# One attention stage in a new static order: maxima moved by DMA, short score tiles merged, one key transpose a group

## The chip, the cores and the metric

The kernel runs on one core of one Trainium2 chip. The metric is the time of one execution in microseconds, taken on the device; several executions are taken, and their median counts. The core has five engines with instruction streams of their own: TensorE (PE), VectorE (DVE), ScalarE (ACT), GpSimd (POOL) and SyncE (SP), which here only issues DMAs. They are ordered among each other by semaphores alone.

## The reference, cut to what matters

Two layers are computed over an input of 8 batches x 512 tokens x 128 features. The change is in the attention of the first:

```python
def _L0_attn_ref(x, Wk, Wq, Wv, Wo, bo, kln_w, kln_b, qln_w, qln_b):
    b, t, e = x.shape              # 8, 512, 128; x is layer-normed before
    h, s = 16, e // 16             # 16 heads of 8
    k = layernorm((x @ Wk).reshape(b, t, h, s), kln_w, kln_b)
    q = layernorm((x @ Wq).reshape(b, t, h, s), qln_w, qln_b)
    v = (x @ Wv).reshape(b, t, h, s)
    dot = einsum('bqhs,bkhs->bhqk', q, k) / sqrt(s)
    attn = softmax(where(causal, dot, -inf), axis=-1)
    return einsum('bhqk,bkhs->bqhs', attn, v).reshape(b, t, e) @ Wo + bo
```

Its result is added to `x` with that of a soft mixture of experts, whose last step (32 tiles of four matmuls, called "out" below) overlaps with the start of the attention. The second layer follows.

## The kernel before

Stage A projects queries, keys and values for all 32 token tiles of 128; stage C is the router and the experts; stage B is the attention. In B the 16 heads of a batch make four groups of four heads, so there are 32 groups in all, and a group has four query tiles and four key tiles of 128 tokens, in two pairs of heads each. For one group these items are done:

- `K`: SP turns the keys by DMA (`turn_keys`, line 656), four transposes of 128 x 256 bf16. The keys were split by POOL before (`nk`, seven steps a batch, lines 813 to 831; `nq` are the same for the queries, `nv` pads the values, `nb` adds the output bias).
- `Q`: PE turns the queries (eight transposes, line 2049), and ACT copies them to `qt1` (line 1652).
- `q` 0 to 7: scores with queries on the partitions, one unit for each query tile and pair of heads (lines 1993 and 1998, the second adds the causal mask); DVE takes each row's maximum from PSUM (`max_q`, line 1149).
- After `q` 7 DVE writes the negated maxima as two bf16 parts into two columns of each head in `qs` (`max_rows`, lines 1156 and 1157).
- `Z`: PE turns `qs` again, now with the maxima in it (line 2049), and ACT copies it to `qt2` (line 1652). The keys have ones in these two columns.
- `k` 0 to 7: scores the other way round, keys on the partitions (line 2009), which hold score minus maximum; ACT takes the exponential (line 1661).
- `m` 0 to 3: POOL zeroes what the causal mask excludes (line 794). `pv` 0 to 3: PE weighs the values (line 2023), ACT copies the sum (line 1667).
- `O`: PE turns the output (line 2062), DVE normalises it into `atok` (lines 1163 and 1168).

Once a batch `A` turns `atok` (line 2062, ACT copies it, line 1652) and `W` multiplies by `Wo` (line 2060); DVE adds the result to `x` and takes the statistics of the new rows (`residual`, lines 1177 to 1190).

PSUM has eight banks. The score units `q` and `k` go round three pairs of banks: PE may write a unit when the unit three places before has been read. `Q`, `Z`, `O`, `A` and `W` all go through bank 6, `pv` sums in bank 7.

The order is written out by hand. Each item has a time, in units of which a group has eight; the items sorted by time are the list, and every engine does its own items of it in that order and waits for each. The list covers two batches (eight groups) and is repeated as a round; items with a time under 16.5 belong to the round before. Before the attention's first round SP and the other engines bring the semaphores up to where a round before would have left them (`Skip`), and POOL's first normalisation waits for SP's.

## Time and profile before

| | us |
|---|---|
| median of 3 runs (lowest, highest) | 1042.38 (1042.19, 1045.29) |
| the profiled execution's own time | 1036.81 |
| span of its trace | 1035.1 |
| from the first to the last group's row maxima (line 1156) | 312.95 |
| mean granted TensorE clock | 0.949 |

The profile is one execution, with the start and length of every instruction on each engine and what released it after a wait. PE is matmuls, PEld the loading of their weights, and SPq the instructions in SP's queue. A busy share is an average over stages with different limits, and an engine's in-order stream means that one late item delays all behind it.

### The profile page before, as it was taken

The page shows a single profiled execution, that of the slowest core. Times are in us where ns is not written, and L with a number is a line of the kernel's source. Part 1 is how long each engine was busy: PE and PEld are TensorE (multiplying, and loading weights), DVE is VectorE, ACT ScalarE, POOL GpSimd, SP SyncE. Part 2 cuts the span into 40 slices and gives each one's busy share as a digit, 9 for nine tenths or more (in the row PEclk, how much of TensorE's full clock was granted, in tenths as well). Part 3 has the DMA queues.
Part 4 walks back from the last instruction along what each step waited for, and adds up shares of the span by engine and source line. Part 5 has one row for each costly group of instructions (what it writes and reads, how often), then busy time and mean ns, then how long its engine had stood idle before and what let it go on. Part 6 is the DMA issues. An engine that isn't in the chain of part 4 may idle for free.

```text
span 1035.1 us, 19063 instructions
## 1 busy us (share of the span) xinstructions
PE 857.0 (83%) x6870; PEld 557.6 (54%) x6870; DVE 708.6 (68%) x1512; ACT 583.8 (56%) x1091; POOL 563.6 (54%) x649
## 2 busy tenths in 40 slices
PE   7699979988899899899898587667888868999880
PEld 4366654467444444444444264345565547998870
DVE  6789963025778788787787459998767754465484
ACT  6566655410877788687787464344776652424220
POOL 2400007182586686686722149996127762888872
PEclk9999999999999999999999789988999998999995
DMA  5012212346111111111110199200101111232287
GB/s 151 1 77 86 83 82 60 95 142 189 23 30 28 24 30 29 24 33 24 28 29 7 50 165 288 61 1 1 41 14 54 43 44 64 87 103 76 75 235 205
DMA packets 111500, 74.59 MB, mean 72 GB/s; under 512 B 42626, under 2 KB 104524, under 8 KB 109360
## 3 DMA queue, kind: packets, MB, share of 16 engines
q1 hardware_dynamic: 101040, 64.05, 22.9%
q0 software_dynamic: 4608, 6.64, 1.9%
q10 hardware_dynamic: 5760, 2.70, 1.0%
q8 instruction: 55, 0.90, 0.4%
q14 instruction: 37, 0.30, 0.1%
HBM read 34.14 MB, written 33.70 MB: 66 GB/s over the span
## 4 chain that ended last, share of the span: by engine, by line
DVE 22%; PE 20%; POOL 14%; issue 11%; ACT 5%; DMA 2%; POOLq 0%; ACTq 0%; DVEq 0%
DVE B_mneg L1149 4%; PE banks L2023 4%; POOL y_dram L976 4%; ACT B_pt L1661 2%; PE banks L1993 2%; PE banks L2049 2%; PE banks L2009 2%; DVE D_dmx L1279 2%; PE banks L2158 2%; PE banks L2107 2%; DVE banks L1328 2%; POOL B_n L818 1%; DVE D_sc L1305 1%; PE banks L2062 1%; POOL x L952 1%
## 5 line engine op out<-in xcount | busy, mean ns | idle before, releaser
L1149 DVE TENSOR_REDUCE B_mneg<-banks 128x2 f32<-128x256 f32 (+3 forms) x256 | 205.4, 822 | 45.1 <-PE banks L1998 36.7
L1661 ACT ACTIVATE B_pt<-banks 128x1024 f32<-128x1024 f32 (+3 forms) x256 | 175.7, 709 | 65.8 <-PE banks L2009 63.6
L794 POOL TENSOR_SCALAR_AFFINE_SELECT B_pt<-B_pt 128x512 f32<-128x512 f32 x128 | 80.9, 634 | 131.3 <-ACT B_pt L1661 123.0
L2023 PE MATMUL banks<-B_pt,B_vp 128*32 128x512 f32 (+3 forms) x1024 | 96.3, 447 | 13.9 <-ACT B_ot L1667 6.9
L1811 ACT ACTIVATE F_gh<-banks 128x512 f32<-128x512 f32 (+1 forms) x96 | 49.4, 527 | 87.2 <-PE banks L2227 83.1
L931 POOL DMA_INDIRECT rows_dram<-F_xs,F_rowi x64 | 62.4, 976 | 59.4 <-issue 58.5
L1652 ACT COPY B_qt<-banks 128x1024 bf16<-128x1024 bf16 x64 | 64.7, 1011 | 40.9 <-PE banks L2049 39.7
L2158 PE MATMUL banks<-D_qk 128*128 128x512 f32 x128 | 74.3, 664 | 12.0 <-DVE D_pr L1290 12.0
L1993 PE MATMUL banks<-B_kt,B_qt 64*128 64x384 bf16 (+3 forms) x512 | 78.6, 304 | 5.1 <-DVE B_mneg L1149 2.5
L2009 PE MATMUL banks<-B_qt,B_kt 64*128 64x256 bf16 (+3 forms) x512 | 77.6, 304 | 4.7 <-ACT B_pt L1661 3.2
L976 POOL DMA_INDIRECT y_dram<-F_yo,F_ide x60 | 60.3, 1004 | 37.6 <-DVE F_yo L1507 17.4
L2235 PE MATMUL banks<-F_gw,F_gh 128*128 128x128 f32 x640 | 75.3, 275 | 0.2 <-DVE F_yo L1507 0.2
L2235 PEld LDWEIGHTS banks<-F_gw,F_gh 128*128 128x128 f32 x640 | 73.9, 192 | 1.1 <-DVE F_yo L1507 0.5
L917 POOL TENSOR_TENSOR D_prodv<-D_gex,D_q 128x64 f32<-128x64 f32 (+7 forms) x64 | 57.0, 933 | 13.2 <-ACT D_gex L1784 13.1
L1998 PE MATMUL banks<-B_mask_q,B_identb 64*128 64x128 bf16 (+1 forms) x512 | 63.6, 202 | 0.0
L1998 PE MATMUL banks<-B_mask_q,B_swapped 64*128 64x128 bf16 (+1 forms) x512 | 61.8, 202 | 0.0
L760 POOL CAST B_identb<-ident 128x128 bf16<-128x128 f32 x1 | 0.3, 290 | 110.3 <-ACT C_slotsT L1600 110.3
L1507 DVE TENSOR_TENSOR F_yo<-banks,F_she 128x512 f32<-128x512 f32 (+1 forms) x24 | 14.5, 602 | 61.9 <-POOL F_ide L961 44.1
L1279 DVE TENSOR_REDUCE D_dmx<-banks 128x1 f32<-128x512 f32 x64 | 43.7, 685 | 17.6 <-PE banks L2158 16.7
L1998 PEld LDWEIGHTS banks<-B_mask_q,B_swapped 64*128 64x128 bf16 x512 | 45.8, 95 | 12.4
L2009 PEld LDWEIGHTS banks<-B_qt,B_kt 64*128 64x128 bf16 x512 | 24.6, 93 | 50.1 <-issue 19.7
L897 POOL TENSOR_TENSOR D_prod<-D_q 128x128 f32<-128x128 f32 (+7 forms) x32 | 44.3, 1413 | 10.3 <-ACT D_q L1711 8.9
(295 smaller groups left out, 2173.7 us busy)
## 6 DMA issues: line engine op xcount, KB each, us to landing
comb_dram<-C_comb SPq DMA_DIRECT2D x8, 1024.0 KB, 3.8
C_cst<-comb_dram SPq DMA_DIRECT2D x8, 1024.0 KB, 5.0
rows_dram<-D_zeros SPq DMA_DIRECT2D x8, 650.0 KB, 15.7
F_xe<-rows_dram SPq DMA_DIRECT2D x8, 650.0 KB, 3.9
C_w<-w_in SPq DMA_DIRECT2D x16, 256.0 KB, 3.1
y_dram<-D_zeros SPq DMA_DIRECT2D x2, 2048.0 KB, 17.7
F_gw<-mw_in SPq DMA_DIRECT2D x16, 256.0 KB, 3.0
F_xs<-y_dram SPq DMA_DIRECT2D x16, 256.0 KB, 4.7
```

The lines of the kernel that those rows point to most:

```text
L794: g.affine_select(out=w, in_=w, compare_op=ALU.is_ge, fill=0.0, base=0, pattern=[[0, G], [1, P]], channel_multiplier=-1).then_inc(B_md, 1)
L976: pool.indirect_dma_start(out=(y_late[late] if late >= 0 else y_dram)[:, :], out_offset=bass.IndirectOffsetOnAxis(ap=ide[:, par, m:m + 1], ...
L1149: v.tensor_reduce(mneg[:, g % 2, qt, 2 * hp:2 * hp + 2], banks2[pair_of_banks(item)][:, :, 0:(qt + 1) * P], X, ALU.max, negate=True).then_ ...
L1279: v.tensor_reduce(dmx[:, u:u + 1], bank[2 + (n - 1) % 3][:], X, ALU.max, negate=True).then_inc(D_mx, 1)
L1652: a.copy(dst, bank[6][:] if kind == "A" else bank[6][:].bitcast(BF16)).then_inc(B_me, 1)
L1661: a.activation(pt[:, 2 * hp:2 * hp + 2, PT_AT[kt]:PT_AT[kt] + w], banks2[pair_of_banks(item)][:, :, 0:w], ACT.Exp).then_inc(B_ex, 1)
L1993: t_.matmul(banks2[ring][:, h, 0:(qt + 1) * P], qt1[HALF[h], g % 2, hp, qt * P:(qt + 1) * P], kt_[HALF[h], g % NG, 0:qt + 1, hp, :], start ...
L1998: ins = t_.matmul(banks2[ring][:, h, qt * P + half * QL:(qt + 1) * P], picks, mask_q[HALF[h], 0:P - half * QL], start=False, stop=(half == 1))
L2009: ins = t_.matmul(banks2[ring][:, h, 0:T - kt * P], kt_[HALF[h], g % NG, kt, hp, :], qt2[HALF[h], g % 2, hp, kt * P:T], start=True, stop=True)
L2023: ins = t_.matmul(bank[7][SL * r:SL * r + SL, kt * P:T], vp[:, g // NG, kt, SL * h:SL * h + SL], pt[:, r, PT_AT[kt]:PT_AT[kt] + T - kt * P ...
L2158: t_.matmul(bank[2 + (n - 1) % 3][:], qk[:, b % 2, h, t * P:(t + 1) * P], qk[:, b % 2, 2 + h, :], start=True, stop=True).then_inc(D_sf, 1)
L2235: ins = t_.matmul(bank[4 + alt][:, t * D:(t + 1) * D], gh[:, alt, m, t * P:(t + 1) * P], gw2[:, e, m, :], start=(m == 0), stop=(m == NJ - 1))
```

## The change

- The repeated round is dropped. One list (`B_PLAN`) holds the items of all 32 groups and the 32 "out" tiles, with new times. `Skip` and its semaphore counts go from this stage, and the key semaphores are waited for at 16 a group and not 64.
- `Z` goes. DVE writes the maxima of a group as 32 bf16 columns into a tile of their own (`mrow`); the new item `R` turns this tile (one transpose), ACT copies 32 partitions of 128 to `mrT`, and SP moves them by four DMAs into the rows of `qt` that stand for the maxima. The first `k` unit waits for these four. `qt` has a place for each of the four groups of a batch.
- The units of query tiles 0 and 1 hold both pairs of heads, and so do those of key tiles 2 and 3: six `q` and six `k` units a group where there were eight of each. The matmuls stay as they are, the maxima and exponentials of such a unit are one instruction.
- `K` is one DMA transpose of 128 x 1024. For this `qs`, `ks`, `vp`, `qkv` and `rst8` are laid out by group, and stage A writes them so.
- `nk` and `nq` have a normalising buffer each, their steps interleave, and the first two batches' steps don't wait for SP.
- In the new list `A` and `W` stand further behind `O`. `st` is written by the aggregation itself, without the copy of line 1190.

The order of PE in one group's period, by the new times: q5, pv0 (two groups back), q3, k5 (two back), k1 (one back), pv1, q2 (next group), k0, q4, R, pv2, k3, q0, pv3, O (three back), k2, q1, k4, Q (two ahead).

```diff
-OF_GROUP = {"q": (-0.6, 0.4, 2.0, 3.3, 3.7, 4.1, 5.1, 7.0), "k": (11.4, 12.4, 14.3, 15.3, 16.3, 17.6, 18.6, 19.0),
-            "m": (14.8, 17.1, 18.4, 20.4), "pv": (15.8, 18.7, 21.9, 22.3), "K": (-8.7,), "Q": (-4.0,), "Z": (9.9,), "O": (24.1,)}
-OF_BATCH = {"nk": (-34.0, -33.6, -32.8, -31.3, -26.6, -26.3, -23.3), "nq": (-23.1, -20.0, -19.0, -17.6, -16.5, -15.4, -13.6),
-            "nv": (-8.1,), "nb": (-13.5,)}
-OF_LAST_GROUP = {"A": 27.2, "W": 29.7}
+GROUPS = B * NG
+QUNITS = ((0, (0, 1)), (1, (0, 1)), (2, (0,)), (2, (1,)), (3, (0,)), (3, (1,)))
+KUNITS = ((0, (0,)), (0, (1,)), (1, (0,)), (1, (1,)), (2, (0, 1)), (3, (0, 1)))
+UNITS_OF = ((0, 1), (2, 3), (4,), (5,))
+
+OF_GROUP = {"K": (-17.95,), "Q": (-8.22,), "q": (-2.64, -1.48, -3.99, 1.48, -3.76, 0.3), "R": (4.89,),
+            "k": (12.09, 10.22, 14.41, 13.26, 14.95, 17.71), "m": (22.44, 25.29, 27.45, 28.1),
+            "pv": (17.26, 19.83, 21.02, 21.43), "O": (30.16,)}
+OF_BATCH = {"nk": (-29.73, -21.65, -19.43, -16.07, -11.11, -9.19, -8.75),
+            "nq": (-34.65, -34.63, -31.38, -23.28, -21.64, -16.54, -14.54), "nv": (20.36,), "nb": (-0.71,)}
+OF_LAST_GROUP = {"A": 34.63, "W": 41.99}
+OUT_FROM, OUT_STEP = -24.24, 1.115
...
-                    for t in range(NT):
-                        c0 = (g % NG) * 2 * P
-                        sp.dma_start_transpose(kt_[:, g % NG, t], ks[:, g // NG, t, c0:c0 + 2 * P]).then_inc(B_kt[g % NG], 16)
+            def turn_keys(g):
+                b = g // NG
+                if g % NG == 0:
+                    sp.wait_ge(B_ks, b + 1)
+                if g >= NG:
+                    sp.wait_ge(B_s2, B_PLAN.nth("k", *LAST_K[g - NG]))
+                sp.dma_start_transpose(kt_[:, g % NG].rearrange("p t a k -> p (t a) k"),
+                                       ks[:, b % 2, g % NG].rearrange("p t c -> p (t c)")).then_inc(B_kt[g % NG], 16)
+
+            def place_max_rows(g):
+                sp.wait_ge(B_me, B_PLAN.nth("misc", "R", g, 0))
+                for h in range(2):
+                    for part in range(2):
+                        r0, to = (2 * h + part) * 2 * NT, h * QL + MAX_AT + part
+                        sp.dma_start(qt[to:to + 1, g % NG].rearrange("p a t k -> p (a t) k"),
+                                     mrT[r0:r0 + 2 * NT, g % 2, :]).then_inc(B_rw[g % 2], 16)
...
+                if len(pairs) == 2:
+                    v.tensor_reduce(mneg[:, g % 2, :, :, qt_], scores[:, :, 0:2 * w].rearrange("p h (a k) -> p h a k", a=2),
                                     X, ALU.max, negate=True).then_inc(B_mx, 1)
...
-                    rows = qs[:, g // NG, :, :].rearrange("p t (h s) -> p t h s", s=QL)[:, :, G * (g % NG):G * (g % NG) + G, :]
-                    own.link(v.tensor_copy(rows[:, :, :, MAX_AT], mneg[:, g % 2, :, :]))
-                    v.tensor_tensor(rows[:, :, :, MAX_AT + 1], mneg[:, g % 2, :, :], rows[:, :, :, MAX_AT],
-                                    ALU.subtract).then_inc(B_m, 1)
+                low = mneg[:, g % 2].rearrange("p h a t -> p h (a t)")
+                own.link(v.tensor_copy(mrow[:, g % 2, :, 0, :], low))
+                v.tensor_tensor(mrow[:, g % 2, :, 1, :], low, mrow[:, g % 2, :, 0, :], ALU.subtract).then_inc(B_m, 1)
...
-                    own.link(v.tensor_copy(st[:, bass.ds(i0, NT), :], mv[:]))
...
+                elif kind == "R":
+                    if g >= 2:
+                        act.wait_ge(B_rw[g % 2], 64 * (g // 2))
+                    ins = a.copy(mrT[0:8 * NT, g % 2, :], bank[6][:].bitcast(BF16)[0:8 * NT, 0:P])
...
+                if len(pairs) == 2:
+                    a.activation(pt[:, :, PT_AT[kt]:PT_AT[kt] + w].rearrange("p (a h) q -> p h a q", a=2),
+                                 scores[:, :, 0:2 * w].rearrange("p h (a q) -> p h a q", a=2), ACT.Exp).then_inc(B_ex, 1)
...
+                if item == FIRST_K[g]:
+                    pe.wait_ge(B_rw[g % 2], 64 * (g // 2 + 1))
...
+                elif kind == "R":
+                    pe.wait_ge(B_m, g + 1)
+                    ins = t_.transpose(halves[0:8 * NT, 0:P], mrow[:, g % 2].rearrange("p h s r -> p (h s r)"), identb[:])
```

## Rows read from the trace of the kernel before

**Rows 1.** The page, part 1: busy us, share of the span, instructions.

```profile
PE 857.0 (83%) x6870; PEld 557.6 (54%) x6870; DVE 708.6 (68%) x1512; ACT 583.8 (56%) x1091; POOL 563.6 (54%) x649
```

**Rows 2.** Windows: stretch, length, busy of PE, PEld, DVE, ACT, POOL, PEclk, DMA, GB/s.

```profile
396.50:477.20 80.70, 72.34 (x953) 36.35 (x952) 65.36 (x117) 62.01 (x90) 58.09 (x72) 1.00 0.14 28
```

**Rows 3.** Timeline of DVE, line 1156 alone: start us, us.

```profile
252.76 0.21 DVE L1156 CAST B_qs<-B_mneg 128x16 bf16<-128x16 f32 x1
...
396.48 0.21 DVE L1156 CAST B_qs<-B_mneg 128x16 bf16<-128x16 f32 x1
...
405.11 0.52 DVE L1156 CAST B_qs<-B_mneg 128x16 bf16<-128x16 f32 x1
...
423.50 1.10 DVE L1156 CAST B_qs<-B_mneg 128x16 bf16<-128x16 f32 x1
...
437.34 0.20 DVE L1156 CAST B_qs<-B_mneg 128x16 bf16<-128x16 f32 x1
...
565.71 0.20 DVE L1156 CAST B_qs<-B_mneg 128x16 bf16<-128x16 f32 x1
```

**Rows 4.** Timeline of all engines at the end of a batch.

```profile
425.86 0.65 PE L2062 MATMUL banks<-ident,B_atok 128*128 128x128 f32 x4 [0.38 <-DVEq L1171]
...
427.19 1.16 PE L2060 MATMUL banks<-wo,B_aT 128*128 128x128 f32 x8 [0.68 <-ACT B_aT L1652]
...
428.38 0.69 DVE L1177 TENSOR_TENSOR x<-banks,x 128x512 f32<-128x512 f32 x1 [2.07 <-PE banks L2060]
...
429.19 0.62 PE L2049 MATMUL banks<-B_identb,B_qs 128*128 128x128 bf16 x8 [0.63 <-DVEq L1178]
...
431.19 0.69 DVE L1149 TENSOR_REDUCE B_mneg<-banks 128x2 f32<-128x512 f32 x1
```

**Rows 5.** Lines, forms apart, 396.5 to 477.2: busy us, mean ns | idle before.

```profile
L1149 DVE TENSOR_REDUCE B_mneg<-banks 128x2 f32<-128x1024 f32 x16 | 19.5, 1220 | 1.0 <-PE banks L1998 0.2
L1661 ACT ACTIVATE B_pt<-banks 128x1024 f32<-128x1024 f32 x16 | 16.5, 1028 | 1.5 <-PE banks L2009 1.0
L1652 ACT COPY B_qt<-banks 128x1024 bf16<-128x1024 bf16 x16 | 16.2, 1011 | 1.3 <-PE banks L2049 0.9
...
L1149 DVE TENSOR_REDUCE B_mneg<-banks 128x2 f32<-128x512 f32 x16 | 11.1, 692 | 8.4 <-PE banks L1998 8.4
...
L1661 ACT ACTIVATE B_pt<-banks 128x512 f32<-128x512 f32 x16 | 8.9, 595 | 13.4 <-PE banks L2009 13.4
...
L1149 DVE TENSOR_REDUCE B_mneg<-banks 128x2 f32<-128x256 f32 x16 | 6.7, 422 | 1.5 <-DVE B_atok L1168 0.5
...
L1661 ACT ACTIVATE B_pt<-banks 128x256 f32<-128x256 f32 x16 | 6.2, 386 | 0.6 <-PE banks L2009 0.5
...
L1156 DVE CAST B_qs<-B_mneg 128x16 bf16<-128x16 f32 x9 | 4.3, 480 | 0.3
```

**Rows 6.** Timeline of PE: the eight transposes and what follows, and one pv.

```profile
400.60 0.62 PE L2049 MATMUL banks<-B_identb,B_qs 128*128 128x128 bf16 x8
...
401.16 0.34 PE L1993 MATMUL banks<-B_kt,B_qt 64*128 64x384 bf16 x2
...
408.08 0.85 PE L2023 MATMUL banks<-B_pt,B_vp 128*32 128x384 f32 x8
```

**Rows 7.** DMA issues: count, KB each, median us from issue to landing.

```profile
B_kt<-B_ks SPq DMA_TRANSPOSE x128, 2.4
...
D_lam<-lams_in SPq DMA_DIRECT2D x4, 64.0 KB, 2.7
```

**Rows 8.** Tile B_kt: ns min/median/max of one issue in SP's queue.

```profile
L656 SPq DMA_TRANSPOSE B_kt<-B_ks x128: 1167/1246/2573, 212.9 to 543.7; - x128
```

**Rows 9.** Timeline of SP behind the attention.

```profile
589.26 1.85 SPq L672 DMA_DIRECT2D D_lam<-lams_in  x4
```

**Rows 10.** Timelines of POOL and PE before the attention.

```profile
203.38 1.07 POOL L813 TENSOR_TENSOR B_n<-qkv,rst 128x512 f32<-128x512 f32 x1 [26.92 <-SPq L135]
...
219.53 7.38 PE L1965 MATMUL banks<-C_eo,C_cst 128*128 128x128 f32 x64 [0.97 <-ACT C_eo L1639]
```

More of the change, by code:

```diff
@@ L209 @@
 OUT_FIRST = sum(bank_ < 4 for bank_ in OUT_BANK)
-def b_items(first, last):
-    if first:
-        return FIRST_ROUND
-    return [item for item in B_ROUNDS.order if not (last and item in EARLY)]
 def pair_of_banks(unit):
-    return B_ROUNDS.streams["unit"].index(unit) % 3
+    return B_PLAN.streams["unit"].index(unit) % 3
 OF_ROUTER = {"g": (-5.3,), "x": (-3.6,), "l": (-0.6, -0.3, 0.5, 0.6), "u": (1.2, 4.2, 3.0, 8.1),
@@ L381, in build @@
         eps, root = sb("eps", [P, 1]), sb("root", [P, 1])
-        turns = sem("turns")
         s_x = [sem(f"x_in{c}") for c in range(4)]
@@ new lines, in residual @@
+            def residual(b, stats=True):
+                dve.wait_ge(B_mf, B_PLAN.nth("misc", "W", b, 0))
+                dve.wait_ge(B_bo, b + 1)
+                i0 = b * NT
+                xb = x[:, i0:i0 + NT, :].rearrange("p t d -> p (t d)")
+                own.link(v.tensor_tensor(xb, bank[6][:], xb, ALU.add))
+                dve.sem_inc(B_me, 1)
+                if not stats:
+                    return
+                for t in range(NT):
+                    ins = v.bn_stats(bn6[:, t, :], x[:, i0 + t, :])
+                own.link(ins)
+                for t in range(NT):
+                    ins = v.bn_aggr(st[:, i0 + t, :], bn6[:, t, :])
+                own.link(ins)
@@ L1228, in second_deviations_of @@
                 own.link(v.reciprocal(rst2[:, tiles], var2[:, tiles]))
-            dve_round(-1, True)
-            for it in range(B // 2 - 1):
-                dve_round(it, False)
-            dve_round(B // 2 - 1, False, True)
+            for item in B_PLAN.order:
+                kind, g, i = item
+                if kind == "out":
+                    add_experts(g, i)
+                elif kind == "q":
+                    max_q(g, i)
+                    if item == LAST_Q[g]:
+                        max_rows(g)
+                elif kind == "O":
+                    normalise(g)
+                elif kind == "W" and g == B - 1:
+                    deviations_of(FIRST_BATCHES, 1)
+                    residual(g, stats=False)
+                elif kind == "W":
+                    residual(g)
             dve.sem_inc(B_end, 1)
@@ new lines, in weigh_values @@
+            def weigh_values(item):
+                _, g, kt = item
+                pe.wait_ge(B_md, B_PLAN.nth("m", "m", g, kt))
+                if kt == 0:
+                    if g % NG == 0:
+                        pe.wait_ge(B_v, g // NG + 1)
+                    if g:
+                        pe.wait_ge(B_ot, g)
+                for r in range(G):
+                    ins = t_.matmul(bank[7][SL * r:SL * r + SL, kt * P:T],
+                                    vp[:, g // NG % 2, g % NG, kt, SL * r:SL * r + SL],
+                                    pt[:, r, PT_AT[kt]:PT_AT[kt] + T - kt * P], start=(kt == 0), stop=(kt == NT - 1))
+                ins.then_inc(B_pv, 1)
@@ new lines, in _ @@
+            pe.wait_ge(B_const, 1)
+            for item in B_PLAN.order:
+                kind, g, i = item
+                if kind == "out":
+                    sum_experts(g, i)
+                elif kind == "q":
+                    scores_q(item)
+                elif kind == "k":
+                    scores_k(item)
+                elif kind == "pv":
+                    weigh_values(item)
+                elif kind in ("Q", "R", "O", "A", "W"):
+                    through_bank_6(item)
```

549 lines of the change are left out of this document (212 added, 337 removed).

## Prediction

> **What bounds the kernel now.** The page came first [rows 1]: PE is busy for 83% of the span, DVE for 68%, and no other engine leads, so the split by stage decides. The windows over the attention of stage 1 show it as periodic: a stretch of 80.70 us, eight groups, has PE busy for 72.3, DVE for 65.4, ACT for 62.0 and POOL for 58.1, at a granted clock of 1.00, and the stretch before it is the same to 0.2 us [rows 2]. PE is idle for 8.4 us of the 80.7, and no engine is full. So it is a schedule in which four engines between 72% and 90% wait for each other in turn, and what the change is worth is read from its rhythm, not from one engine's load.
>
> The rhythm is in the timeline of DVE: line 1156 runs once a group, when the row maxima of the group are complete [rows 3]. The first is at 252.76 and the last at 565.71 us, 31 intervals in 312.95 us, 10.10 us a group. The two intervals from 405.11 to 423.50 take 18.39, 9.2 each; those in which a batch is finished take longer: 423.50 to 437.34 is 13.84. The one of the batch before ends at 396.48; as the round is 80.70 and its other six intervals are 8.6 to 9.3 (the two shown, and the one of 8.63 from 396.48 to 405.11), it takes about 12.4. Batch ends thus cost about 3.3 and 4.8 us over an ordinary interval of 9.07, 8.1 us a round.
>
> The timeline of the 13.84 us interval says why [rows 4]: A (atok turned, line 2062) starts at 425.86, W (the projection, line 2060) at 427.19 after a wait of 0.68 for the copy of A's result, the residual on DVE at 428.38 after DVE has sat idle for 2.07, and the next Q (line 2049) at 429.19 after another 0.63. O, A, W and the residual stand next to each other in the order of PE and share bank 6, so all queued behind them waits: scores, then maxima, then exponentials.
>
> **The change, part by part.**
>
> *The end of a batch.* In the new list O stands at 30.2, A at 34.6 and W at 42.0, where it was 24.1, 27.2 and 29.7 (a group is 8 of these units). Other units of work now lie between each, so the waits of [rows 4] go, and the work itself stays. On PE that is A (0.65) and W (1.1 to 1.2), on DVE 2.8 us from the residual at 428.38 to the next maximum at 431.19 [rows 4]. The copy of line 1190 and its gap go from that. I leave 2.2 us for each batch end, DVE's part, since DVE and PE are both near the path. So 8.1 us a round becomes 4.4: 1.85 us for each of the 7 batch ends inside the stretch, 13.0 us. Bounds: nothing, if the new order makes another wait, and 4.05 x 7 = 28 us, if this work hides as well.
>
> *Z goes, R comes.* Z turned the queries a second time, with the maxima in them. Eight transposes take PE from 400.60 to the next matmul at 401.16, 0.56 us [rows 6], and ACT copies 1,024 columns in 1.01 us [rows 5]. R is one transpose (0.07, an eighth) and a copy of 128 columns on 32 partitions: between nothing and the 0.39 of the shortest exponential (256 columns); I take 0.3. PE gains 0.49 us a group, ACT 0.7.
>
> *Merged units.* Of the sixteen units of a group four go. DVE: 2 x 0.422 becomes 0.692, 2 x 0.692 becomes 1.220, 0.32 us less. ACT: 2 x 0.595 becomes 1.028, 2 x 0.386 becomes 0.595, 0.34 us less [rows 5]. The matmuls are as many as before. With a ring of three bank pairs PE hands over twelve times and not sixteen. The CAST of line 1156 means 0.48 and once took 1.10 [rows 3, 5], against 0.21 at its shortest; I give it no gain, with at most 0.27 us a group as its other bound.
>
> What a group gains in time: no single engine is the path, so the least relief of the three bounds what is sure (DVE 0.32) and the relief of PE (0.49) is the rate at which it can go on when fed. The fewer hand-overs add something that no row prices. I take 0.5 us a group, 31 x 0.5 = 15.5 us. Bounds: 0, if the waits keep their pattern; and, if PE never idles, a round of 72.2 - 8 x 0.49 = 68.3 us, that is 12.4 less than 80.70 for both parts together, 48 us over 31 groups.
>
> *The maxima by DMA.* Behind R and its copy SP issues four DMAs of 2 KB, and the first k of the group waits for all. Four issues in a row on SP took 1.85 us [rows 9]. Their landing isn't in the trace in this form; the nearest rows are 2.4 us (the key transposes, also from SBUF to SBUF) and 2.7 (64 KB from HBM) [rows 7]. Chain: transpose 0.2, on ACT up to 1.0 behind an exponential, copy 0.3, three issues 1.4, landing 2.4 from the start of the fourth issue: 5.3 us. In the new order thirteen of a group's eighteen pieces of PE work lie between R and that k. Outside it are only k, pv 1, q, k, q: one pv of 0.85 [rows 6] and four units of about 0.3 (the two matmuls of one took 0.34 in the row of 384 columns), 2.0 us. At 8.6 us a group (9.07 less 0.5) that leaves 6.6 us. 5.3 is hidden, with 1.3 us to spare, so I cost it at nothing. Uncovered it costs PE its lateness in every group. The Trainium skill, DMA: Bandwidth & Descriptors, section Anatomy of one DMA, puts the fixed part of a DMA at about 2.0 us (its fit is of DMAs issued by GpSimd); by it the chain would be an estimated 4.9 us, and the room 1.7.
>
> *One key transpose for four.* An issue occupies SP for 1.246 us in the median, four for 5.0 [rows 8]. One of four times the size takes between 1.25 and 5.0 us. Nothing waits for it soon: it is issued when the fourth group back has finished its k units (unit 17.7 - 32 = -14.3), and the first q is at -4.0, ten units or some 11 us later. But it stands on SP ahead of the next R. That R's copy is ready some 3.5 us after the k unit that releases the transpose, so with 5 us of issue R is 1.5 us late, with 1.25 not at all. I take nothing; at 5 us the 1.3 us to spare just about goes.
>
> *Head and tail.* POOL starts the first normalisation at 203.38 after 26.92 us in wait for SP; the new order drops that wait, but PE begins the 32 expert tiles only at 219.53 [rows 10] and they run as many as before, so this is worth 0. In the order both have about the same number of units ahead of the first k; I take 0 there, plus or minus 3. At the end no q is left to hide the last R: its chain is 5.3 us where Z's was 0.62 and 1.01 [rows 5, 6], 3.7 more, part of it under what is left of group 30. I add 2.0. Stage A writes the same elements in another layout, 0.
>
> *POOL* keeps its work, 58.1 us of a round of 73 [rows 2]. It would be the next bound after PE.
>
> Sum: -13.0 - 15.5 + 2.0 = -26.5 us. The profiled execution took 1036.81 us (span 1035.1), so 1010.3; it lay 5.6 under the median of 1042.38, and against the median this is **1016 us**. The round should be 80.7 - 3.7 - 4.0 = 73.0 us.
>
> **The rivals.**
>
> *The full gain.* PE waits hardly at all, rounds near 70 us. For: the waits of [rows 4] are most of its idle time. Against: DVE and POOL are then near 90% of the round. Some 10.7 x 31 / 8 = 41 less, with the tail 39: 1003 us, down to 994.
>
> *Only the batch ends.* The order has its waits elsewhere, ordinary intervals stay at 9.07. For: ring and in-order waits, not load, set them. -13.0 + 2.0: 1031 us.
>
> *No net change*, POOL's masks come late behind the normalising steps, which the new list puts two at a time between them. For: POOL's busy share rises from 72% to 80%. Against: in the new order pv 0 stands five units behind the k units that its mask needs. 1042 us.
>
> *The maxima are late (slower).* Place: the first k of each group, waiting for the four DMAs. It decides when the chain is over 6.6 us by more than 0.9: the other gains are then used up, 26.5 / 31. So at a chain of 7.5 us, 2.2 more than my sum: landings of 4.6 us, or 3 us behind the transpose and 1.5 us of slower issue together. At 8.3 us it is 1.7 x 31 = 53 less 26.5, 1068 us. Against: no landing of a small transfer in the trace is over 2.7 [rows 7]. For: nothing like a write of eight rows into one partition is in it. The Trainium skill, DMA: Bandwidth & Descriptors, section Queues, rings and completion order, says that descriptors of one ring are consumed in order: the rows' would then stand behind the keys' of the same queue. No run here shows that.
>
> **How the numbers follow.** Forecast 0.40 (1007 to 1024), full gain 0.20, batch ends only 0.20, no change 0.07, late maxima 0.13. The range, 994 to 1041, takes in the first three and leaves out 0.20. Within 0.3%, 3.1 us, is about what a measurement of this kernel can't tell from no change. Faster 0.80, same 0.07, slower 0.13.
>
> **What the profile after would show.** The intervals between row maxima: 8.6 ordinary, about 10.8 at a batch end. A round at PE 68, DVE 61 to 63, ACT 54, POOL 57 busy. No wait of PE for the rows' DMAs but in the last group, and PE not waiting between A and W. DMA rows: issue to landing near 2.4 for the maxima; one transpose on SP of 1.25 to 5 us. Wrong would be: PE waiting for a DMA at the k line in each group, or ordinary intervals of 9 us with the masks as releaser.

## The result, and the profile after

The changed kernel takes 981.91 us in the median of 4 runs (978.41 to 987.38), the kernel before 1042.29 in the runs beside it (4, 1039.33 to 1045.29): ratio 0.9425, interval 0.9368 to 0.9483, 60 us less. The forecast was 1016 and its range began at 994, so the sign was right and the size was not: the sum had 26.5 us and the range at most 48. Each trace is of one execution, and the one to be read with care is that of e5_merge_old_order below, a slow execution of 1117.36 us where its fast ones take 1091 to 1098, but at a granted clock of 1.00 in the stage and with its excess behind the last mark, where it has 532 us and the other experiments 509 to 519.

The spans of the two profiled executions, 1035.1 and 976.7, differ by 58.4. The row maxima, the mark of [rows 3], say where that lies (timeline of DVE of the changed kernel, line 1119 alone: start, duration):

```profile
250.89 0.17 DVE L1119 CAST B_mrow<-B_mneg 128x16 bf16<-128x16 f32 x1
...
350.72 0.18 DVE L1119 CAST B_mrow<-B_mneg 128x16 bf16<-128x16 f32 x1
...
359.98 0.45 DVE L1119 CAST B_mrow<-B_mneg 128x16 bf16<-128x16 f32 x1
...
367.69 0.45 DVE L1119 CAST B_mrow<-B_mneg 128x16 bf16<-128x16 f32 x1
...
375.90 0.28 DVE L1119 CAST B_mrow<-B_mneg 128x16 bf16<-128x16 f32 x1
...
383.92 0.18 DVE L1119 CAST B_mrow<-B_mneg 128x16 bf16<-128x16 f32 x1
...
507.75 0.45 DVE L1119 CAST B_mrow<-B_mneg 128x16 bf16<-128x16 f32 x1
```

31 intervals in 256.86 us, 8.29 us a group, where there were 312.95 and 10.10: 56.1 of the 58.4 us are inside the stage. The first mark is 1.9 us earlier, and from the last mark to the end of the span it is 469.0 us where it was 469.4. The repeating batch is 9.26, 7.71, 8.21 and 8.02: an ordinary group takes 7.98, and a batch end costs 1.28 over that. In before these were 9.07 and 4.05. In the terms of the forecast's sum: ordinary groups 34 us (forecast 15.5), batch ends 19.4 (13.0), and the rest, 5 us, at and beyond the two ends of the stage.

The windows over eight groups, to be set beside [rows 2] (length, then busy of PE, PEld, DVE, ACT, POOL, the granted clock, DMA share, GB/s):

```profile
334.50:400.90 66.40, 63.26 (x900) 31.81 (x896) 62.57 (x99) 54.28 (x75) 56.76 (x65) 1.00 0.21 35
```

The round was to be 73.0 us and is 66.4. It is even below the 68.3 that I gave as the round in which PE never idles, and PE still idles 3.1 of it. PE and DVE are now busy for 95% and 94%. On the page of the whole span PE went down by 37 us from [rows 1]:

```profile
PE 820.4 (84%) x6646; PEld 538.7 (55%) x6646; DVE 694.8 (71%) x1441; ACT 551.9 (57%) x1027; POOL 558.3 (57%) x617
```

The lines of this stretch with forms apart (busy us, mean ns, idle just before them), beside [rows 5]:

```profile
L1112 DVE TENSOR_REDUCE B_mneg<-banks 128x2 f32<-128x1024 f32 x16 | 19.4, 1214 | 0.0
...
L1109 DVE TENSOR_REDUCE B_mneg<-banks 128x4 f32<-128x1024 f32 x8 | 9.8, 1226 | 1.2
...
L1623 ACT ACTIVATE B_pt<-banks 128x1024 f32<-128x1024 f32 x8 | 8.1, 1018 | 0.0
L1603 ACT COPY B_qt<-banks 128x1024 bf16<-128x1024 bf16 x8 | 8.1, 1018 | 0.0
...
L1109 DVE TENSOR_REDUCE B_mneg<-banks 128x4 f32<-128x512 f32 x8 | 5.4, 678 | 0.0
...
L1623 ACT ACTIVATE B_pt<-banks 128x512 f32<-128x512 f32 x8 | 4.8, 597 | 3.2 <-PE banks L1952 3.2
```

The joined tiles last as long as the sum said: 1,226 and 678 ns for the two joined maxima, 1,018 and 597 for the two joined exponentials. The idle time before the 512-column forms, 8.4 us on DVE and 13.4 on ACT in [rows 5], is 0.0 and 3.2.

The end of a batch, beside [rows 4] (timeline of all engines):

```profile
341.97 0.66 PE L1996 MATMUL banks<-ident,B_atok 128*128 128x128 f32 x4
...
349.73 1.16 PE L1999 MATMUL banks<-wo,B_aT 128*128 128x128 f32 x8
...
351.03 0.68 DVE L1140 TENSOR_TENSOR x<-banks,x 128x512 f32<-128x512 f32 x1
```

No row has a wait: the 0.68 before W and the 2.07 before the residual are gone. And the maxima on their way (timeline of PE, ACT and SP of one group):

```profile
344.21 0.23 PE L1989 MATMUL banks<-B_identb,B_mrow 128*32 128x128 bf16 x1
...
344.94 0.24 ACT L1607 COPY B_mrT<-banks 32x128 bf16<-32x128 bf16 x1
...
345.20 2.67 SPq L642 DMA_DIRECT2D B_qt<-B_mrT  x4
...
350.82 0.39 PE L1952 MATMUL banks<-B_qt,B_kt 64*128 64x512 bf16 x2
```

R stands at 344.21, the issue of the fourth DMA begins at about 347.2, and the first k, at 350.82, waits for nothing. The view of line 642 and the tile view of the keys (ns min/median/max of one issue; then who waited, us and times):

```profile
L642 SPq DMA_DIRECT2D B_qt<-B_mrT x128: 634/635/1272, 254.1 to 512.6; - x128
...
  PE banks L1952: 1.4, 3
```

```profile
L634 SPq DMA_TRANSPOSE B_kt<-B_ks x32: 1232/1232/2190, 223.2 to 491.9; - x32
```

PE waits for the maxima's DMAs three times in 32 groups, 1.4 us in all.

### The profile page after: what moved, and what is told of

Its sections match the earlier page's. It is cut to its first block, busy times and chain, and to the rows that moved or that the text cites. A ratio compares the mean times of both kernels' runs of the same rounds, so it can differ in the third digit from the quotient of the medians.

```text
span 976.7 us, 18288 instructions
## 1 busy us (share of the span) xinstructions
PE 820.4 (84%) x6646; PEld 538.7 (55%) x6646; DVE 694.8 (71%) x1441; ACT 551.9 (57%) x1027; POOL 558.3 (57%) x617
## 4 chain that ended last, share of the span: by engine, by line
PE 37%; DVE 25%; POOL 13%; issue 10%; DMA 3%; ACT 3%; SPq 1%; ACTq 0%; POOLq 0%; DVEq 0%
PE banks L1965 5%; POOL y_dram L937 4%; PE banks L1934 3%; DVE B_mneg L1112 3%; PE banks L1952 3%; PE banks L1884 3%; PE banks L1878 2%; PE banks L1911 2%; DVE D_dmx L1228 2%; DVE C_nmax L1050 2%; PE banks L1856 2%; PE banks L1939 2%; PE banks L2086 2%; DVE banks L1277 2%; PE banks L2035 2%
## 5 line engine op out<-in xcount | busy, mean ns | idle before, releaser
L1112 DVE TENSOR_REDUCE B_mneg<-banks 128x2 f32<-128x768 f32 (+1 forms) x128 | 136.3, 1086 | 7.8 <-PE banks L1939 4.2
L1627 ACT ACTIVATE B_pt<-banks 128x768 f32<-128x768 f32 (+1 forms) x128 | 117.1, 917 | 31.8 <-PE banks L1952 30.0
L1934 PE MATMUL banks<-B_kt,B_qt 64*128 64x256 bf16 (+3 forms) x512 | 72.7, 301 | 1.7 <-ACT B_pt L1627 1.2
L1952 PE MATMUL banks<-B_qt,B_kt 64*128 64x256 bf16 (+3 forms) x512 | 64.7, 300 | 8.5 <-DVE B_mneg L1112 5.3
L1109 DVE TENSOR_REDUCE B_mneg<-banks 128x4 f32<-128x512 f32 x64 | 61.0, 953 | 4.8 <-PE banks L1939 0.5
L1623 ACT ACTIVATE B_pt<-banks 128x1024 f32<-128x1024 f32 x64 | 51.5, 809 | 12.7 <-PE banks L1952 12.7
L1939 PE MATMUL banks<-B_mask_q,B_identb 64*128 64x128 bf16 (+1 forms) x512 | 58.4, 202 | 0.0
L1939 PE MATMUL banks<-B_mask_q,B_swapped 64*128 64x128 bf16 (+1 forms) x512 | 57.1, 202 | 0.0
L1934 PEld LDWEIGHTS banks<-B_kt,B_qt 64*128 64x128 bf16 x512 | 24.8, 94 | 56.3 <-DVE B_mneg L1109 25.2
```

The source lines that it names most:

```text
L1112: v.tensor_reduce(mneg[:, g % 2, :, pairs[0], qt_], scores[:, :, 0:w], X, ALU.max, negate=True).then_inc(B_mx, 1)
L1627: a.activation(pt[:, 2 * hp:2 * hp + 2, PT_AT[kt]:PT_AT[kt] + w], scores[:, :, 0:w], ACT.Exp).then_inc(B_ex, 1)
L1934: t_.matmul(scores[:, h, n * w:(n + 1) * w], qt[HALF[h], g % NG, hp, qt_, :], kt_[HALF[h], g % NG, 0:qt_ + 1, hp, :], start=True, stop=False)
L1939: ins = t_.matmul(scores[:, h, n * w + qt_ * P + half * QL:(n + 1) * w], picks, mask_q[HALF[h], 0:P - half * QL], start=False, stop=(half ...
L1952: ins = t_.matmul(scores[:, h, n * w:(n + 1) * w], kt_[HALF[h], g % NG, kt, hp, :], qt[HALF[h], g % NG, hp, kt:NT, :], start=True, stop=True)
```

## The experiments

Fifteen kernels. Where they ran, the kernel before takes 1091 to 1096 us and not 1042, and the changed kernel 1022 (e8) and not 982. The extra time is not in the attention stage: there the changed kernel keeps its rhythm (8.28 and 8.29 us a group), and behind the last mark e8 has 517 us at a granted clock of 0.86, where the first trace had 469 at 0.90. So each ratio is against before on the same chip, and what tells the kernels apart best is the mean interval between row maxima, in us a group. A difference in it, times 31, is what it makes inside the stage.

Three cautions. Before was not traced there, so its 10.10 is that of the first trace; the ratios lie 0 to 1.6% below what the intervals give (e1, with 10.08 us a group, has 0.988), and what before loses there isn't explained. The experiments are best compared with each other. The granted clock of the stage is 1.00 in most of these kernels, but 0.98 in e13, 0.97 in e4, 0.96 in e2, 0.95 in e14 and 0.86 in e15, so a part of what these lose can be the clock. And all fifteen keep the changed kernel's layout by group and its normalising buffers; "old" is the order and the work alone.

| kernel | order | units a group | us a group | ratio (interval) |
|---|---|---|---|---|
| before | old, by rounds | 16 | 10.10 | 1 |
| e1_one_list_old | old, one list | 16 | 10.08 | 0.988 (0.982 to 0.994) |
| e5_merge_old_order | old, one list | 12 | 10.51 | 1.006 (1.001 to 1.011) |
| e14_split_later | old, later half moved | 16 | 13.22 | 1.089 (1.081 to 1.096) |
| e13_joined_later | old, later half moved | 12 | 11.47 | 1.029 (1.020 to 1.037) |
| e15_new_work_old_times | old, new work | 12 | 13.76 | 1.100 (1.091 to 1.109) |
| e2_old_work_new_order | new | 16 | 10.91 | 1.016 (1.010 to 1.023) |
| e4_split_new | new | 16 | 10.82 | 1.010 (1.005 to 1.015) |
| e11_join_q_only | new | 14 | 9.57 | 0.983 (0.972 to 0.995) |
| e9_split_spread | new, halves apart | 16 | 9.48 | 0.982 (0.971 to 0.993) |
| e10_five_spare | new | 12 | 8.93 | 0.967 (0.954 to 0.980) |
| e3_z_added | new | 12 | 8.64 | 0.952 (0.945 to 0.959) |
| e12_aw_tight | new, A and W close | 12 | 8.47 | 0.952 (0.941 to 0.963) |
| e6_two_drains | new | 12, drained in two | 8.35 | 0.935 (0.923 to 0.947) |
| e7_two_spare | new | 12 | 8.33 | 0.941 (0.929 to 0.952) |
| e8_changed_again | new | 12 | 8.28 | 0.932 (0.921 to 0.944) |

**The list, and the order.** The first four kernels undo parts of the change. e1 is the old work at the old times, sorted into one list without rounds:

```
-B_ROUNDS = Rounds(item_times(), AHEAD, PG, 8 * PG, {
+B_PLAN = Plan(b_item_times(), {"unit": "qk", "q": "q", "k": "k", "m": "m", "pv": ("pv",), "misc": "QROAW"})
```

> The old work (second turn Z, sixteen units a group, four key transposes) and the old times, but in one list for all 32 groups. Theory A, that the edge of the repeated round is what sets A and W of every second batch side by side at the end of the list: the intervals of 13.8 us become 12.4, four of them, about 1036 us, ordinary intervals stay at 9.1. Theory B, that the edge costs nothing: 1042 us and the same intervals as before.

10.08 us a group: nothing inside the stage. The batch end, by turns 13.84 and about 12.4 us before, is 12.25 in the repeating batch, and the other groups take 8.62, 9.89 and 9.53, where they had 9.07 on average: what the edge gives comes back as longer groups. e2 puts the old amount of work into the new order:

```
-QUNITS = ((0, (0, 1)), (1, (0, 1)), (2, (0,)), (2, (1,)), (3, (0,)), (3, (1,)))
+QUNITS = KUNITS = tuple((t, (hp,)) for t in range(4) for hp in range(2))
+                    for k in range(1, 2 * NT):
+                        t_.transpose(halves[:, k * P:(k + 1) * P], swapped[:], identb[:])
+                    ins = a.copy(unused[:, P:], bank[6][:].bitcast(BF16)[:, P:])
+                for t in range(NT):
+                    sp.dma_start_transpose(kt_[:, g % NG, t], ks[:, b % 2, g % NG, t, :]).then_inc(B_kt[g % NG], 16)
```

> The changed kernel with the old work put back: sixteen units a group (the halves of a merged unit next to each other), four key transposes, and seven more transposes and a copy of 896 columns at R, of a constant, in place of what Z did; the maxima still go by DMA. If the order makes most of the gain (theory order): 8.9 to 9.3 us a group with batch ends in it, 1005 to 1020 us. If the work taken out makes most of it (theory work): 9.8 a group, 1030 to 1035.

10.91 us a group, slower than before. It falls outside both theories (8.9 to 9.3, and 9.8). The new order without the new work is worth less than nothing when the halves of a short tile stand side by side; e9 below moves them apart.

**The work of Z.** e3 keeps the changed kernel and adds what Z had over R: seven more transposes (of a constant) and a copy of 896 columns.

> The changed kernel with seven more transposes on PE (of a constant) and a copy of 896 columns on ACT at R, the work of the second turn Z. If PE is the path: 0.48 us a group and more, 997 to 1000 us. If DVE is: at most 0.2 a group, 982 to 988.

8.64 against 8.28: 0.36 us a group, 11 us, between the two theories. In the sum it was a part of the 0.5 that I took for a group, with 0.49 of relief on PE. This price holds in the changed kernel only: e2 has this work and the four key transposes over e4 (next), and takes 0.1 us a group more.

**The joined tiles.** e4 is the changed kernel with sixteen units, both halves of a short tile side by side, and all else as changed.

> The changed kernel with sixteen units a group, the halves of each merged unit next to each other in the list. By my prediction's sum (DVE 0.32, ACT 0.34, PE nothing): about 10 us more, 992. If merging also relieves PE, as the fall of its busy time by 1.1 us a group says: 16 to 25 us more, 998 to 1007.

10.82 us, where the two theories expected 10 and 16 to 25 us: against its own split the joining is worth 2.53 us a group, 78 us, more than the whole change. e4's windows (as above), its chain of units (timeline of all engines) and its waits of PE (waited for: us, times, longest):

```profile
300.00:400.00 100.00, 79.58 (x1017) 38.69 (x1015) 77.25 (x128) 65.08 (x103) 63.23 (x73) 0.97 0.15 26
```

```profile
343.38 0.61 PE L1933 MATMUL banks<-B_kt,B_qt 64*128 64x512 bf16 x2
...
344.19 1.23 DVE L1111 TENSOR_REDUCE B_mneg<-banks 128x2 f32<-128x1024 f32 x1 [1.56 <-PE banks L1938]
...
345.64 0.96 DVE L1111 TENSOR_REDUCE B_mneg<-banks 128x2 f32<-128x768 f32 x1 [0.23 <-PE banks L1938]
...
346.66 0.39 PE L1951 MATMUL banks<-B_qt,B_kt 64*128 64x512 bf16 x2 [0.95 <-DVE B_mneg L1111]
...
350.38 0.23 PE L1933 MATMUL banks<-B_kt,B_qt 64*128 64x128 bf16 x2 [0.54 <-DVE B_mneg L1111]
```

```profile
PE banks L1951 <- DVE B_mneg L1111: 9.5, 9, 1.7
PE banks L1933 <- DVE B_mneg L1111: 5.0, 9, 0.7
PE banks L1951 <- ACT B_pt L1626: 4.3, 9, 0.5
```

Over the whole stage the 2.53 us are 1.73 of more idle time on PE and 0.80 of more busy time (its granted clock means 0.97). No engine is full, and PE stands for 18.8 us of 100 until DVE or ACT has drained a pair of banks. At 346.66 the wait ends 0.06 us after the maximum at 345.64 does. The same gaps return in each group. (The Trainium skill, Perfetto Trace Analysis, section Optimization Strategy, says of such a gap that it "can mean there isn't enough SBUF/PSUM for the next tile to be allocated (buffer count, tile sizes)"; here the trace agrees, with the releasers above.)

Is it the places in the ring or the instructions? e6 leaves the joined tiles in one pair of banks but drains them by two instructions, as before:

```
-                    v.tensor_reduce(mneg[:, g % 2, :, :, qt_], scores[:, :, 0:2 * w].rearrange(...), X, ALU.max, negate=True)
+                    for hp in range(2):
+                        ins = v.tensor_reduce(mneg[:, g % 2, :, hp, qt_], scores[:, :, hp * w:(hp + 1) * w], X, ALU.max, negate=True)
```

(and likewise for the exponential).

> The changed kernel, its short tiles still joined in one bank pair, but the joined unit read by two maxima on VectorE and two exponentials on ScalarE, one for each head pair, as before had them. So the instructions of the kernel before are back on both engines (four more a group) and the places in the ring are as in the changed kernel. Theory A, that instructions are what the joining saves: as slow as the split kernel, some 10.8 us a group, 1.01 of before. Theory B, that places and hand-overs are what it saves: the four instructions cost at most what they are, 0.3 us a group, so 8.3 to 8.7 us a group and 0.94 to 0.955 of before.

8.35 us, 0.07 over the changed kernel, or 2 us of 1,000. Its window is that of the changed kernel, PE 95% busy:

```profile
300.00:400.00 100.00, 95.12 (x1337) 47.05 (x1334) 94.75 (x171) 82.33 (x135) 85.48 (x98) 1.00 0.20 35
```

So the instructions, the one thing that I had priced, are worth 0.07 us a group here, and what is left of the 2.53 goes with the unit's place in the ring. Two things come with that place and aren't told apart here: its hand-over (e6 still signals once a unit), and that PE writes four matmuls in a row, which takes it less busy time (see the floor below). Two more kernels share this out. e9 has sixteen units again, with the second halves moved away from the first:

```
-            "q": (-2.64, -2.64, -1.48, -1.48, -3.99, 1.48, -3.76, 0.3)
-            "k": (12.09, 10.22, 14.41, 13.26, 14.95, 14.95, 17.71, 17.71)
+            "q": (-2.64, -0.6, -1.48, -0.2, -3.99, 1.48, -3.76, 0.3)
+            "k": (12.09, 10.22, 14.41, 13.26, 14.95, 18.9, 17.71, 19.3)
```

> The changed kernel with sixteen units a group as in e4_split_new (1.010 of before, 10.82 us a group), but the second halves of the four formerly joined short tiles are moved away from the first, into the stretches of the order that hold few units (query tiles 0 and 1: 2.0 and 1.3 us behind their first halves, mirror tiles 2 and 3: 4.0 and 1.6 us behind). Theory A, four more places taken in a ring of three cost their hand-overs wherever they stand: 10.3 us a group or more, 0.99 or more. Theory B, only the two short halves side by side stall it, since they give TensorE nothing to do while VectorE and ScalarE drain: 8.3 to 9.3 us a group, 0.935 to 0.965. Half way, 9.3 to 10.3, would leave both a part.

> The changed kernel with query tiles 0 and 1 joined as it has them and mirror tiles 2 and 3 in two units each, side by side: fourteen units a group. Splitting both cost 2.5 us a group (e4_split_new). Theory A, each place of the ring costs the same: +1.25 us a group, 9.5 us, 0.97 to 0.98 of before. Theory B, the long chain of the mirror tiles (ScalarE drains them at 0.7 to 1.2 us, and waits for the maxima) is what the split hits: +2 us or more, 10.3 us, 0.99 or more. Theory C, the query side: +0.5 us at most.

e9 takes 9.48 us: half of the cost goes when the halves stand apart, half stays (0.78 of idle time on PE and 0.42 of busy time). Sixteen units in this order are thus 0.6 us a group faster than before. e11, with two of the four joins undone, takes 9.57, half of e4's loss: what its first theory said, the same price a place (0.96 idle, 0.32 busy). The waits of PE in e9 and e11, in 100 us each:

```profile
PE banks L1933 <- ACT B_pt L1626: 7.0, 13, 0.6
PE banks L1951 <- DVE B_mneg L1111: 3.9, 12, 0.5
```

```profile
PE banks L1952 <- DVE B_mneg L1112: 9.7, 11, 1.0
PE banks L1952 <- ACT B_pt L1627: 4.1, 10, 0.4
```

**Joined tiles in the old order.** e5 is e1 with twelve units:

```
-            "q": (-0.6, 0.4, 2.0, 3.3, 3.7, 4.1, 5.1, 7.0), "k": (11.4, 12.4, 14.3, 15.3, 16.3, 17.6, 18.6, 19.0)
+            "q": (-0.1, 2.6, 3.7, 4.1, 5.1, 7.0), "k": (11.4, 12.4, 14.3, 15.3, 16.9, 18.8)
```

> The work of the kernel before (whole query tiles turned behind the maxima, four key transposes a group), its order times, one list for all groups, and short tiles 2 and 3 of the first matrix and short tiles 0 and 1 ... of the mirror image joined: six units and six units where before had eight and eight. To be set beside e1_one_list_old, which differs from it only in the joining (0.988 of the kernel before, 10.08 us a group). Theory A, the joining is worth its instructions only (some 0.34 us of ScalarE and 0.32 of VectorE a group, under 0.4 us a group): 0.975 to 0.99 of before, 9.6 to 10.1 us a group. Theory B, the joining frees places in the ring of three bank pairs that the score tiles pass through, and these hand-overs set the pace in any order: 8.7 to 9.3 us a group, 0.93 to 0.95 of before. Theory C, it frees them but only the new order can use it: 9.4 to 10.0 us a group here.

10.51 us, slower than e1 and outside all three theories; the whole times agree in direction, 1093 us against 1086. PE's waits in 100 us:

```profile
PE banks L1979 <- DVEq L1122: 8.1, 10, 1.4
PE banks L1952 <- ACT B_ot L1622: 3.8, 7, 0.5
```

It doesn't wait for the ring, but for the row maxima at Z (line 1979). I took the chain behind the last query tile for the cause, and gave it more room in e13 and e14: Z later by 0.7, mirror tiles and all that follows by 1.2.

> e5_merge_old_order (old work and old order times, short tiles joined, 10.51 us a group) with everything behind the maxima later in the order: R by 0.7 of the eight units of a group, mirror tiles, their products with V, the output transposes and what follows by 1.2. In e5 TensorE waited at R for the maxima of the last query tile, 8.1 us in 100, and hardly for the ring. Theory A, the old order cannot use joined tiles because this chain ends last in it: with more room for it 9.2 to 10.0 us a group. Theory B, the joined units are bad in the old order by where they stand in it: 10.3 us or more.

> The same shift for the kernel with sixteen units (e1_one_list_old, 10.08 us a group), in which TensorE waited at R for only 2.6 us in 100 and for the ring for 3.9. Theory A, here the ring is the edge and the chain is not: 9.9 to 10.1 us, no gain. If it falls as much as e13, the room behind R was worth the time in either case, and joining is not what makes use of it.

The theory behind the two fell. The shift costs 1.0 us a group with joined tiles (11.47) and 3.1 without (13.22, where 9.9 to 10.1 was expected): with split tiles PE now waits for pairs of banks for 24.6 us in 100, with joined ones for 8.3. In e13 the wait at Z is down to 3.5 us in 100, and another has come first, that of the products with V for the masks:

```profile
PE banks L1951 <- POOL B_pt L767: 5.5, 4, 1.9
...
PE banks L1978 <- DVEq L1121: 3.5, 9, 0.4
```

So the chain was not what to relieve. e13's 11.47 lies where the second theory had it, but not for its reason: the joined units are not what is bad in that order, since between e14 and e13, otherwise the same, joining is worth 1.75 us a group.

**The way of the maxima.** e7 and e10 put two and five spare DMAs of 2 KB, to DRAM, ahead of the four on SP, so that these are issued 1.3 and 3.2 us later.

```
+                for i in range(2):
+                    sp.dma_start(spare[2 * g + i], mrT[0:2 * NT, g % 2, :]).then_inc(B_sp[g % 2], 16)
```

> The changed kernel with two spare DMAs of 2 KB on SyncE's queue, in each group, ahead of the four that move the maxima: at 0.635 us an issue they land 1.3 us later. Theory A, the chain of the maxima has some 3 us left before the first mirror tile: nothing (0.94 to 0.95, 8.3 us a group). Theory B, the chain is the edge already in each group: +1.3 us a group on 31 groups, some +40 us, 0.98.

> The changed kernel itself once more, so that the others of this call have it on their chip: 0.937 to 0.948 of before, 8.29 us a group, by every theory.

> As e7_two_spare (which took 8.33 us a group against 8.28 without them) with five spare DMAs ahead of the four that move the maxima: these land 3.2 us later. Theory A, the chain of the maxima has some 3 us left: 0 to +0.7 us a group, so under +20 us. Theory B, the slack is about 1.3 us, and everything beyond it goes into each group: +1.9 us a group, +60 us, 0.99 of before.

8.33 and 8.93 us: 1.3 us of lateness cost 0.05 us a group, 3.2 us cost 0.65. The waits of PE in e10, in 100 us, show the edge reached in five of some eleven groups:

```profile
PE banks L1959 <- DVE B_mneg L1118: 5.7, 6, 1.0
PE banks L1959 <- DMA B_qt<-B_mrT: 4.9, 5, 1.4
```

e15 has the new work at the old times, with the first k only 1.5 behind R.

> The work of the changed kernel whole (joined tiles, one key transpose, the maxima alone turned and moved by DMA) in the order times of before, in which the first mirror tile stands 1.5 behind R in place of 5.3. The four DMAs with their copy take some 3.9 us to the landing. Theory A, a late landing goes into each group almost whole, as my slower rival had it: 11 to 12 us a group, 1.01 to 1.06 of before. Theory B, TensorE finds other work and half of it is hidden: 10 to 11 us.

13.76 us a group, 3.7 more than before, beyond what either theory allowed. The chain in the open (timelines of PE and SP, then PE's waits in 100 us):

```profile
339.34 0.23 PE L1988 MATMUL banks<-B_identb,B_mrow 128*32 128x128 bf16 x1 [0.42 <-DVEq L1132]
...
340.14 3.09 SPq L641 DMA_DIRECT2D B_qt<-B_mrT  x4
...
344.44 0.47 PE L1951 MATMUL banks<-B_qt,B_kt 64*128 64x512 bf16 x2 [3.38 <-DMA B_qt<-B_mrT]
```

```profile
PE banks L1951 <- DMA B_qt<-B_mrT: 23.1, 8, 3.4
```

From R to k it takes 5.10 us. Over the whole stage this wait comes 32 times and takes 90.8 us, 2.8 us a group. In this kernel the granted clock also means 0.86 over the stage, so the 3.7 us are not all the wait itself.

**A and W.** e12 moves both close behind the last O again, as they were.

```
-OF_LAST_GROUP = {"A": 34.63, "W": 41.99}
+OF_LAST_GROUP = {"A": 33.26, "W": 35.76}
```

> The changed kernel, with the transposes of the attention result and the product with the output weights put back close behind the transposes of the last group (1.4 and 2.5 us between the three instead of 4.5 and 7.4), as before had them at the end of a batch. My prediction held that this row of turns through one bank costs 3.6 us of a batch end, 13 us with the round's edge for all of them. Theory A, it does: +2 to +3.5 us a batch, +15 to +28 us. Theory B, with one list other work lies between them in any case: under +1 us a batch, within 0.7% of the changed kernel.

8.47 us, 0.19 us a group or 6 us for all batch ends, 0.8 a batch: its second theory. But its four intervals are 7.47, 7.46, 9.55 and 9.52, so its batch ends cost 4.1 us over an ordinary group, as in before, and its ordinary groups are half a microsecond shorter than the changed kernel's. Read so, moving A and W apart mostly spreads the same delay over the batch. The waits come back (timeline of PE), but they are small:

```profile
344.48 0.66 PE L1996 MATMUL banks<-ident,B_atok 128*128 128x128 f32 x4 [1.16 <-ACT B_qt L1603]
```

## Why the prediction was wrong, step by step

**The step that failed** is the price of the merged units: "The fewer hand-overs add something that no row prices. I take 0.5 us a group." I priced the joining by its instructions and took the hand-overs for a small addition. It is the other way round. e6 puts the instructions at 0.07 us a group; e4, e9 and e11 put the four places of the ring at 2.5 us with the halves side by side, 1.2 with them apart. That alone is 37 to 78 us, where the sum had 15.5 for everything a group gains, and where ordinary groups did gain 1.09 us each, 34 us. The instructions were oversized as well: I took 0.32 us a group on DVE and 0.34 on ACT from the rows, and e6 has 0.13 and 0.12 more of them (busy time by form, whole stage).

Why a place is dear can be seen in e4, though only as an estimate. A large query tile is filled from 343.38 and drained at 345.42 (344.19 and 1.23): it holds its pair for 2.04 us. The ring has three pairs, so the fourth unit finds a free pair without waiting only if three units take at least that long to pass. By an estimate from the measured rhythm, three of twelve units pass in 3/12 x 8.29 = 2.07 us, three of sixteen would pass in 3/16 x 8.29 = 1.55. So twelve units just fit at the changed kernel's pace, and for sixteen three places last 2.0 us at 3/16 x 10.8, the pace of e4. This is no limit that was measured: 2.04 us is one large unit and not the mean, and e9 runs sixteen units at 9.48 us, 1.78 for three of them. It says that the ring is tight, not where it ends, and that where short and long units stand matters as much. What shows the ring at work is PE's waits, 18.8 us of 100 in e4 and 10.9 in e9. In before they are small, so there the ring is not what sets the pace (waits of PE, 300 to 400 us):

```profile
PE banks L2023 <- POOL B_pt L794: 2.8, 5, 0.8
PE banks L2049 <- DVEq L1171: 2.4, 9, 0.3
...
PE banks L1993 <- DVE B_mneg L1149: 0.8, 1, 0.8
...
PE banks L2009 <- DVE B_mneg L1149: 0.7, 2, 0.3
```

It comes up when the order is made denser. The eight banks leave no room for a fourth pair, so a longer ring, the direct test, was not run.

**The order and the joining don't add up.** The old order with joined tiles is 10.51 (as I placed them), the new order with split ones 10.82 or, with the halves apart, 9.48, both together 8.29, neither 10.08. A sum of parts, each priced in the kernel before, can't find 56 us of which one part has nothing alone and the other 19 at best (e9, with Z's work already gone). Here the parts were costed as independent, and that is the error behind the number. Shown is that the 8.29 needs both; the twelve-unit versions of the old order that I tried (e5, e13) had their waits at the row maxima and at the masks, and that no good order with the old spacing of maxima and mirror tiles exists isn't shown.

**The floor** was wrong as well: "if PE never idles, a round of 72.2 - 8 x 0.49 = 68.3" (with the 72.34 of [rows 2] it is 68.4). PE's busy time fell by 9.1 us a round, 1.13 a group, not 0.49. "The matmuls are as many as before" was true and didn't mean that their busy time is. The lines of PE over 300 to 400 us, first before, then after:

```profile
L2009 PE MATMUL banks<-B_qt,B_kt 64*128 64x512 bf16 (+3 forms) x160 | 24.3, 303 | 0.7 <-DVE B_mneg L1149 0.7
L1993 PE MATMUL banks<-B_kt,B_qt 64*128 64x512 bf16 (+3 forms) x156 | 23.9, 303 | 1.0 <-DVE B_mneg L1149 0.8
```

```profile
L1934 PE MATMUL banks<-B_kt,B_qt 64*128 64x384 bf16 (+3 forms) x194 | 27.6, 301 | 0.0
...
L1952 PE MATMUL banks<-B_qt,B_kt 64*128 64x128 bf16 (+3 forms) x196 | 24.7, 298 | 3.5 <-DVE B_mneg L1112 2.2 <-DMA B_qt<-B_mrT 0.5
```

A group has sixteen of each. One matmul lasts the same, 0.30 us, but they overlap: the sixteen of the mirror image occupied 24.3 / 160 x 16 = 2.43 us and now 24.7 / 196 x 16 = 2.02, those of the queries 2.45 and now 2.28. With some of them four in a row into one pair, they overlap more than two and two; e4, split again in the new order, is back at 21.9 / 148 x 16 = 2.37 for those of the mirror image. That is 0.58 us, and with Z's 0.49 most of the 1.13. (The Trainium skill, Perfetto Trace Analysis, section Identifying the Most-Contended Engine, warns that matmul busy time is no good measure of how near PE is to its limit, since pipelined instructions look smaller in the trace; here the trace agrees.) So the low end of the range rested on a busy share that was no bound, and the round fell through it, 66.4 against 68.3.

**The end of a batch, -13.0:** right in the shape, wrong in the cause. Its excess went from 4.05 to 1.28 us, 19 us over 7 batches. But e12 gives the distance between O, A and W, the mechanism I had named, 6 us, and e1 the single list 0.5 us. In both ordinary groups moved against the batch end: in e12 its excess is back at 4.1 us while they take 7.47, in e1 they took back what the edge gave. So the split of the gain into 34 for groups and 19 for batch ends is not one by cause, and what the batch ends gained beyond these 6.5 us isn't assigned to one.

**Z, R and its chain.** 11 us by e3, 0.36 us a group where PE's relief was put at 0.49. Chain: 5.3 us in the sum, 5.10 in e15. Its parts erred in opposite directions: from R to the first issue it is 0.80 us (340.14 less 339.34) where I took 1.5, an issue is 0.635 us where I took 0.46 from [rows 9], so the three ahead of the last take 2.45 and not 1.4, and the landing behind the start of the fourth issue is 1.85 us where I took 2.4 from [rows 7] (344.44, less the fourth issue's start at 340.14 + 3.09 - 0.64 = 342.59). The 1.3 us to spare hold: e7 uses them up for 0.05 us a group. 3.2 us of lateness cost 0.65, a third of what lies beyond 1.3. "No wait of PE for the rows' DMAs but in the last group" came out as three waits of 1.4 us together.

**The late maxima,** the slower rival, has its mechanism confirmed and its condition not met: where the order leaves the chain in the open (e15), PE waits for it in each of the 32 groups and the kernel takes 3.7 us a group more than before, some 114 us. The chance was for a landing that didn't come.

**The key transpose, 0:** right as far as is shown (no run has it alone; with Z's work it is worth 0.1 us a group between e2 and e4). One issue for four costs 1.232 us, as one did before. **Head, 0 plus or minus 3:** 1.9 us earlier. **Tail, +2.0:** -0.4; the last R's chain was hidden but for 0.55 us of wait, at 514.42 us. **POOL:** no wait of PE worth naming for its masks, 85% busy.

**What the rows of before did say.** In [rows 5] DVE idled 8.4 us just before the maxima of 512 columns, out of 15.3 idle in all, and ACT 13.4 of 18.7 before the exponentials of the same size. In the changed kernel the idle time sits there no more. I had both numbers on the page, used only the durations beside them, and so read a queue of units as a set of loads. That they point to the ring is only argued: in e4, with no fewer units, the idle time of DVE moved to the large tiles, and the ring was short all the same.

None of the other fourteen is faster than the changed kernel.

## What to carry to other kernels

When tiles pass from one engine to others through a few shared buffers, count the buffers beside the engines: so many units a period, each holding a buffer from the first write to the end of the drain, against the number of buffers times the period. The count warns that the ring is tight; the waits in a trace say whether it is. Joining two short units paid here by the place it frees and not by the instruction it saves, and only in the order that was short enough for that place to be missed; so a new order and a new unit size are priced together or not at all. Busy time of matmuls was no floor here, since the same matmuls with more of them in a row took less of it.

## What the runs showed of the hardware

- Four DMAs of 2 KB from SBUF to SBUF are issued on SP at 0.635 us each, over a third more than the 0.46 of those in [rows 9], and the wait for them ends 1.85 us after the start of the last issue (e15, one group).
- A DMA transpose of the four key tiles of a group in one instruction holds SP for 1.232 us, the same as one of a quarter of the size (1.246 in [rows 8]), and its landing is 3.1 us in the median against 2.4.
- Two maxima for each joined one cost VectorE 0.13 us of busy time a group (two such tiles), two exponentials ScalarE 0.12, and the kernel 0.07 us (e6), with VectorE busy for 95% there and 93% in the changed kernel beside it (300 to 400 us).
- Sixteen matmuls of 0.30 us occupied TensorE for 2.43 us two by two (before), 2.37 split in the new order (e4) and 2.02 with eight of them four in a row (after).
